# The residual of a state-space block: added by GpSimd in SBUF, or by an identity matmul in the projection's PSUM bank

## The chip, the core and the metric

The kernel runs on one core of a Trainium2 chip. The metric is the device time of one execution in microseconds; of the kernel before it is the median of three runs. A profile is one further execution, recorded by the hardware profiler; its span and its own time are given apart from the median.

## The reference, cut to what matters

Three blocks stand in a row on an input of 4 batches x 1024 positions x 256 channels, all in f32: a gated feed-forward block with three cycles, a state-space (Mamba) block, and the feed-forward block again.

```
x = x + 0.5 * ffn(layernorm(x))
x = x + attn(layernorm(x))
x = x + 0.5 * ffn(layernorm(x))

def attn(resid, ...):                     # resid = layernorm(x)
    xn = resid * rsqrt(mean(resid**2) + eps) * norm_w
    skip, x = xn @ skip_w.T, xn @ in_w.T  # 512 channels each
    x = silu(causal_conv4(x))
    delta = softplus(x @ wd1.T @ wd2.T + wd2_b);  B = x @ wB.T;  C = x @ wC.T
    h[t] = exp(delta[t] * A) * h[t-1] + (delta[t] * x[t]) * B[t]     # 16 states
    y = sum_n h[t, n] * C[t, n] + W_D * x
    y = y * silu(skip)
    return resid + y @ out_w.T
```

So after the state-space block x becomes x + layernorm(x) + y @ out_w.T. The sum of the last two additions is what the change moves.

## The kernel before

The residual stream lies in SBUF all the time as `x_tok`, 32 tiles of 128 positions x 256 channels. The state-space block (function `mamba`) works through 8 segments of 512 positions, numbered i = 0 to 7, two to a batch; the second one of a batch (odd i) starts from the state that the first one left. A segment has 32 units, K = 32 i + k: 16 states n for the first half of the channels and 16 for the second. One unit is, on two channel groups of 128 x 512:

- ScalarE: exp(delta * A) into the PSUM pair `a_bank` (L848, `decay`), and in even segments a copy of the last column (L860)
- GpSimd (POOL): `u` = dx * B (L969, `drive`), up to four units ahead of the scan (a ring of four buffers)
- VectorE (DVE): the scan along the positions (L1065), and in 11 of 16 states the product with C (L1077, result `hc`); in the other five, n = 0, 3, 6, 9, 12, the scan writes `hid` and POOL forms the product (L981, result `hc_pool`)
- TensorE (PE): adds the products over n in the PSUM pair `y_bank` by matmuls with the identity (L1229).

Between the units stand the steps that prepare the next segment and finish the last one. Every engine is programmed by a loop over K, and the tables `AT` and `PLACES` say in which unit k of a segment a step is issued. No scheduler moves anything: an engine does its list in order and waits on semaphores. These steps matter here:

- k = 1, DVE `finish` (L1087) multiplies `y_bank` by the gate for the second channel half of the segment before; with that its `y` is complete.
- k = 2, PE starts the next sum with `feed_through` (L1217), which waits for that `finish`, and then does the output projection of the segment before (kind "out", L1206): for c = 0 (k = 2) and c = 1 (k = 3) two tiles of 128 positions each, 4 matmuls of 256 columns per tile, into one of the two work banks `w_bank`.
- k = 4 and 5, ScalarE `take_out` (L942) copies the bank, 128 x 512, into the scratch `th`.
- k = 7 and 8, POOL `out_add` (L1008) adds `th` to two tiles of `x_tok`.
- k = 5, 6, 8, 9, PE does the input projection of the next segment (kind "in", L1192), k = 7 to 11 ScalarE (L901, L903) takes it out of the bank, and from k = 6 on DVE convolves it (L1100, `convolve`).
- k = 6 and 9, ScalarE `standardise` (L870) replaces x by x + layernorm(x) in `x_tok` for the next segment (semaphore `z`).

The number k tells in which turn of an engine's own loop a step is issued; ScalarE and POOL run ahead of DVE, and PE runs behind it.

An f32 matmul shows as two records in the trace, so the 16 matmul calls of one "out" of a segment are 32 records. After the last segment a drain turn (i = 8) does `finish`, "out", `take_out` and `out_add` for segment 7, with nothing else to do but statistics on DVE; then all engines meet at a barrier, and the second feed-forward block starts.

Of the kernel before, what the change touches and what calls it, by code (L numbers as in the profile page):

```python
# [14 lines left out]
ALU = mybir.AluOpType  # L15
ACT = mybir.ActivationFunctionType
AX = mybir.AxisListType

P = 128
# [606 lines left out]
def mamba(nc, mem, bc_rows):  # L626
# [52 lines left out]
        "dx": (30, 6),  # L679
        "out_add": (7, 8),  # L680
    }

    def due(k, kind):

        return [c for c, t in enumerate(AT[kind]) if t == k]
# [7 lines left out]
    def puts_out(i):  # L693
        return i >= 1
# [41 lines left out]
    with ExitStack() as ctx:  # L736
# [45 lines left out]
            "brow0", "brow1", "brow2", "crow0", "crow1", "crow2",  # L782
            "u", "a", "scan", "carry", "hc", "hc_pool", "y_dve", "y_pool", "y", "out_there", "out_added")}
        block = ctx.enter_context(nc.Block())
# [5 lines left out]
        def col(key, c, n=1):  # L790
            o = W512[key][0]
            return w512[:, c, o:o + n]
# [32 lines left out]
        def _(act):  # L825
# [105 lines left out]
            def gate_half(i, c):  # L931
                b = work_there((i, "skip", c))
                if c == 0:
                    act.wait_ge(S["out_added"], 2 * i)
                if c >= 2:
                    act.wait_ge(S["gated"], i * KE + c - 1)
                nc.scalar.activation(th[:, c % 2, :], b, ACT.Tanh, scale=0.5).then_inc(S["tanh_s"], 1)

            def take_out(i, c):
                b = work_there((i, "out", c))  # L940
                act.wait_ge(S["gated"], i * KE)
                nc.scalar.activation(th[:, c, :], b, ACT.Copy).then_inc(S["out_there"], 1)  # L942

# [15 lines left out]
        def _(pool):  # L959
# [42 lines left out]

            def out_add(i, g):

                pool.wait_ge(S["out_there"], 2 * (i - 1) + g + 1)
                pool.wait_ge(S["z"], 2 * i)
                at = (i - 1) * HT + 2 * g
                nc.gpsimd.tensor_tensor(x_tok[:, at:at + 2, :], x_tok[:, at:at + 2, :],  # L1008
                                        th[:, g, :].rearrange("p (a d) -> p a d", d=DIM),
                                        ALU.add).then_inc(S["out_added"], 1)  # L1010

            for K in range(-UNITS, TOTAL + UNITS):
                i, k = K // UNITS, K % UNITS
                if core(i):
                    drive(K)
                if 0 <= K - WEIGH_LAG < TOTAL and by_pool(K - WEIGH_LAG):
                    weigh(K - WEIGH_LAG)
                for g in due(k, "out_add") if puts_out(i) else ():
                    out_add(i, g)
                if core(i):  # L1020
                    softplus(i, 1, k)
                if prep(i):
                    softplus(i + 1, 0, k)

        @block.vector
        def _(dve):
# [135 lines left out]

            dve.wait_ge(S["out_added"], 2 * 2 * HALVES)
            for t in range(2 * BT):
# [7 lines left out]
        def _(pe):  # L1172
            pe.wait_ge(S["diag_d"], 1)

            def work(i, kind, c, part):
# [23 lines left out]
                elif kind == "dt":  # L1199
                    pe.wait_ge(S["proj"], p + 1)  # L1200
                    op = nc.tensor.matmul(b, w64[:, c * P:(c + 1) * P], proj[0:RANK, :], start=True, stop=True)
                elif kind == "out":
                    pe.wait_ge(S["y"], KE * i)
                    for d in range(KE):
                        at = (2 * c + part) * P
                        op = nc.tensor.matmul(b[:, part * DIM:(part + 1) * DIM], gate[:, d, at:at + P],  # L1206
                                              col("out", d, DIM), start=d == 0, stop=d == KE - 1)
                if part == len(PLACES[kind][c]) - 1:
# [95 lines left out]
```

## Time and profile before

| | |
|---|---|
| median of 3 runs | 1491.64 us (1488.38 to 1492.56) |
| the profiled execution | 1491.21 us, its span 1489.4 us |
| busy share of the span | DVE 88%, PE 77%, POOL 69%, ScalarE 52% |
| the state-space block | about 235 to 1288 us of the span |
| one segment in the middle | about 124.5 us |
| "out" matmuls, copies, POOL additions | 256 records, 16 and 16 |

The span is the time in which the engines work; the 1.8 us between it and the execution's time lie outside. Busy shares are means over stages: the feed-forward blocks at both ends are bound otherwise than the eight segments.

### The profile page before, as it was taken

What the parts mean: (1) busy time and instruction counts of PE and PEld (TensorE: products, weight loads), DVE (VectorE), ACT (ScalarE), POOL (GpSimd) and SP (SyncE); (2) the same over time, 40 slices, a digit from 0 to 9 for tenths busy, and PEclk for the clock granted to TensorE, in tenths of its full rate; (3) what the DMA queues carried; (4) which work ended last, traced back from release to release, by engine and by line L of the source; (5) the groups of instructions that cost most, each with busy time, mean ns of one, the idle gap of its engine ahead of it and who ended that gap; (6) DMA issues with size and microseconds to landing.
All of it is one profiled execution on the core that took longest, in us unless ns stands there. A gap on an engine that the chain in (4) does not pass through costs nothing. (4 is left out here: it accounts for less than half of the span.)

```text
span 1489.4 us, 11591 instructions
## 1 busy us (share of the span) xinstructions
PE 1140.8 (77%) x3072; PEld 537.1 (36%) x3072; DVE 1308.7 (88%) x1793; ACT 776.0 (52%) x1348; POOL 1032.9 (69%) x470
## 2 busy tenths in 40 slices
PE   2979965469687787867868777786887677798996
PEld 2545442123242242333324324232432322454544
DVE  5897894499999989999998999999899899789777
ACT  1544434656754655764565575466557334254443
POOL 1241310698997899899799799879979999224131
PEclk8999986589998998998999899799989989799998
DMA  5000000334434433443343443344344443000001
GB/s 184 0 1 0 0 1 14 115 113 149 161 116 136 148 128 128 142 141 114 128 146 125 141 141 115 139 143 141 114 143 142 141 153 115 1 0 1 29 29 57
DMA packets 46945, 146.53 MB, mean 98 GB/s; under 512 B 4448, under 2 KB 13280, under 8 KB 46880
## 3 DMA queue, kind: packets, MB, share of 16 engines
q1 hardware_dynamic: 46384, 144.96, 29.4%
q10 hardware_dynamic: 496, 0.82, 0.2%
q8 instruction: 25, 0.41, 0.1%
q14 instruction: 40, 0.33, 0.1%
HBM read 141.05 MB, written 4.72 MB: 98 GB/s over the span
## 5 line engine op out<-in xcount | busy, mean ns | idle before, releaser
L969 POOL TENSOR_TENSOR m_u<-m_dx,m_brow 128x1024 f32<-128x1024 f32 x256 | 599.1, 2364 | 36.4 <-DVE m_a_bank L1065 36.3
L1229 PE MATMUL m_y_bank<-m_hc,ident 128*128 128x512 f32 x704 | 382.4, 673 | 188.5 <-DVE m_hc L1077 188.5
L848 ACT ACTIVATE m_a_bank<-m_delta,m_negA 128x512 f32<-128x512 f32 x512 | 335.1, 684 | 174.7 <-DVE m_hc L1077 136.8
L188 POOL TENSOR_TENSOR f_state_lo<-f_state,f_state_hi 128x512 fp32r<-128x512 f32 (+1 forms) x64 | 122.4, 1925 | 251.8 <-DVE f_state_hi L202 251.8
L1229 PEld LDWEIGHTS m_y_bank<-m_hc,ident 128*128 128x128 f32 x704 | 135.3, 207 | 419.1 <-DVE m_hc L1077 293.8
L1065 DVE TENSOR_TENSOR_SCAN m_a_bank<-m_a_bank,m_carry,m_u 128x512 f32<-128x512 f32 x176 | 216.7, 1281 | 12.4 <-POOL m_u L969 12.4
L1077 DVE TENSOR_TENSOR m_hc<-m_a_bank,m_crow 128x512 f32<-128x512 f32 x352 | 224.5, 684 | 0.0
L981 POOL TENSOR_TENSOR m_hc_pool<-m_hid,m_crow 128x1024 f32<-128x1024 f32 x80 | 189.1, 2363 | 49.0 <-DVE m_hid L1065 48.9
L1065 DVE TENSOR_TENSOR_SCAN m_a_bank<-m_a_bank,m_u 128x512 f32<-128x512 f32 x176 | 206.0, 1220 | 10.6 <-POOL m_u L969 9.7
L1229 PE MATMUL m_y_bank<-m_hc_pool,ident 128*128 128x512 f32 x320 | 151.2, 595 | 0.3 <-POOL m_hc_pool L981 0.3
L1192 PE MATMUL m_w_bank<-m_xn,w 128*128 128x512 f32 x240 | 116.9, 610 | 5.5 <-DVE m_x L1124 5.5
L496 ACT ACTIVATE f_h<-f_bank,w 128x512 f32<-128x512 f32 x96 | 66.2, 690 | 88.5 <-PE f_bank L385 88.4
L1065 DVE TENSOR_TENSOR_SCAN m_hid<-m_a_bank,m_u 128x512 f32<-128x512 f32 x80 | 93.6, 1215 | 14.0 <-POOL m_u L969 12.2
L385 PE MATMUL f_bank<-f_state_hi,f_w_lo 128*128 128x512 f32 x192 | 90.3, 470 | 13.0 <-POOL f_state_lo L188 13.0
L1065 DVE TENSOR_TENSOR_SCAN m_hid<-m_a_bank,m_carry,m_u 128x512 f32<-128x512 f32 x80 | 98.3, 1274 | 0.3
L397 PE MATMUL f_bank<-f_h,w 128*128 128x512 f32 x192 | 92.8, 615 | 0.0
L992 POOL TENSOR_TENSOR m_dx<-m_tmp_u,m_dx 128x1024 f32<-128x1024 f32 x16 | 37.8, 2361 | 73.2 <-ACT m_tmp_u L929 73.2
L1229 PEld LDWEIGHTS m_y_bank<-m_hc_pool,ident 128*128 128x128 f32 x320 | 60.3, 190 | 76.8 <-issue 75.0
L385 PE MATMUL f_bank<-f_state_lo,f_w_hi 128*128 128x512 f32 x192 | 78.6, 409 | 0.0
L385 PE MATMUL f_bank<-f_state_hi,f_w_hi 128*128 128x512 f32 x192 | 78.5, 409 | 0.0
L1100 DVE SCALAR_TENSOR_TENSOR m_dx<-m_w_bank,m_conv,m_dx 128x511 f32<-128x511 f32 (+2 forms) x84 | 62.5, 744 | 13.9 <-ACT m_dx L903 12.8
L860 ACT ACTIVATE m_carry<-m_a_bank 128x2 f32<-128x2 f32 x88 | 15.0, 171 | 113.6 <-DVE m_hc L1077 113.6
(132 smaller groups left out, 1606.1 us busy)
## 6 DMA issues: line engine op xcount, KB each, us to landing
m_brow<-bc_rows SPq DMA_DIRECT2D x128, 512.0 KB, 4.8
m_crow<-bc_rows SPq DMA_DIRECT2D x128, 512.0 KB, 4.0
x_tok<-x_in SPq DMA_DIRECT2D x4, 1024.0 KB, 8.7
out<-x_tok SPq DMA_DIRECT2D x3, 1024.0 KB, 4.4
w<-w_in SPq DMA_DIRECT2D x1, 1024.0 KB, 12.3
out<-x_tok SPq DMA_DIRECT2D x2, 512.0 KB, 3.0
w<-w_in SPq DMA_DIRECT2D x1, 750.0 KB, 10.3
w<-w_in ACTq DMA_DIRECT2D x1, 512.0 KB, 6.0
```

The lines of the kernel that those rows point to most:

```text
L188: nc.gpsimd.tensor_tensor(state_lo[:, :, cs], state[:, :, cs], state_hi[:, :, cs].bitcast(F32), ALU.subtract).then_inc(split, 1)
L385: last = nc.tensor.matmul(bank[h * 2 + m][:, :], wt[:, k, m * P:(m + 1) * P], st[:, k, cs], start=n == 0, stop=n == len(passes) - 1)
L397: last = nc.tensor.matmul(bank[4 + h][:, :], w(w256, W256, "w2", k), h1[:, k, h * BANK:(h + 1) * BANK], start=k == 0, stop=k == KD - 1)
L496: nc.scalar.activation(h1[:, m, h * BANK:(h + 1) * BANK], bank[h * 2 + m][:, :], ACT.Gelu, bias=w128[:, o:o + 1]).then_inc(h1_ready, 1)
L848: nc.scalar.activation(a_bank[K % 2][:, j, :], delta[:, i % 2, c, :], ACT.Exp, scale=negA[:, c, n:n + 1]).then_inc(S["a"], 1)
L969: nc.gpsimd.tensor_tensor(u[:, K % U_RING, :, :], dx[:, i % 2, 2 * q:2 * q + 2, :], brow[:, K // 2 % ROW_RING, K % 2, :].unsqueeze(1).to_b ...
L981: nc.gpsimd.tensor_tensor(hc_pool[:, before % POOL_RING, :, :], hid[:, before % POOL_RING, :, :], crow[:, K // 2 % ROW_RING, K % 2, :].uns ...
L1065: nc.vector.tensor_tensor_scan(hid[:, pool_before(K) % POOL_RING, j, :] if by_pool(K) else a, a, u[:, K % U_RING, j, :], 0.0 if i % 2 == 0 ...
L1077: nc.vector.tensor_tensor(hc[:, before % HC_RING, j, :], a_bank[K % 2][:, j, :], crow[:, K // 2 % ROW_RING, K % 2, :], ALU.mult).then_inc( ...
L1100: nc.vector.scalar_tensor_tensor(a[:, s:], b[:, 0:BANK - s], conv[:, c, k:k + 1], a[:, s:], ALU.mult, ALU.add)\
L1192: op = nc.tensor.matmul(b, w256[:, part, o:o + P], xn[:, (p if kind == "in" else i) % 2, part, :], start=part == 0, stop=part == KD - 1)
L1229: op = nc.tensor.matmul(y_bank[:, j, :], ident[:, :], source[:, before % ring, j, :], start=False, stop=K % PASS == POOL_N[-1])
```

## The change

The addition on POOL goes. PE writes the two `x_tok` tiles into the output projection's bank first, by one matmul with the identity for each tile (start=True), and the four matmuls of the projection add to them (start=False). ScalarE's copy then goes from the bank straight into `x_tok`, over the old value. The four identity matmuls of a segment have the shape of the others in this bank: 128 x 128 weights, 256 columns, f32. The semaphore `out_added` goes; what waited for it (the gate's tanh on ScalarE, the final statistics on DVE) waits for `gated` or `out_there`. The wait for `z` moves from POOL's addition to PE's first identity matmul.

```
-        "out_add": (7, 8),
...
             def gate_half(i, c):
                 b = work_there((i, "skip", c))
-                if c == 0:
-                    act.wait_ge(S["out_added"], 2 * i)
-                if c >= 2:
+                if i > 0 or c >= 2:
                     act.wait_ge(S["gated"], i * KE + c - 1)
...
             def take_out(i, c):
                 b = work_there((i, "out", c))
-                act.wait_ge(S["gated"], i * KE)
-                nc.scalar.activation(th[:, c, :], b, ACT.Copy).then_inc(S["out_there"], 1)
+                at = (i - 1) * HT + 2 * c
+                nc.scalar.activation(x_tok[:, at:at + 2, :], b.rearrange("p (a d) -> p a d", d=DIM), ACT.Copy)\
+                    .then_inc(S["out_there"], 1)
...
-            def out_add(i, g):
-
-                pool.wait_ge(S["out_there"], 2 * (i - 1) + g + 1)
-                pool.wait_ge(S["z"], 2 * i)
-                at = (i - 1) * HT + 2 * g
-                nc.gpsimd.tensor_tensor(x_tok[:, at:at + 2, :], x_tok[:, at:at + 2, :],
-                                        th[:, g, :].rearrange("p (a d) -> p a d", d=DIM),
-                                        ALU.add).then_inc(S["out_added"], 1)
...
-            dve.wait_ge(S["out_added"], 2 * 2 * HALVES)
+            dve.wait_ge(S["out_there"], 2 * 2 * HALVES)
...
                 elif kind == "out":
+                    at = (2 * c + part) * P
+                    if part == 0:
+                        pe.wait_ge(S["z"], 2 * i)
+                    nc.tensor.matmul(b[:, part * DIM:(part + 1) * DIM], ident[:, :],
+                                     x_tok[:, (i - 1) * HT + 2 * c + part, :], start=True, stop=False)
                     pe.wait_ge(S["y"], KE * i)
                     for d in range(KE):
-                        at = (2 * c + part) * P
                         op = nc.tensor.matmul(b[:, part * DIM:(part + 1) * DIM], gate[:, d, at:at + P],
-                                              col("out", d, DIM), start=d == 0, stop=d == KE - 1)
+                                              col("out", d, DIM), start=False, stop=d == KE - 1)
```

In the lists below a MATMUL row is one matmul call, and x3 means three alike. On PE, at the units 2 and 3 of a segment, the list before reads:

```order
L1217 MATMUL m_y_bank<-m_x,m_diag_d 128x512 [waits m_y]
L1217 MATMUL m_y_bank<-m_x,m_diag_d 128x512
L1229 MATMUL m_y_bank<-m_hc,ident 128x512 [waits m_hc]
L1229 MATMUL m_y_bank<-m_hc,ident 128x512
L1206 MATMUL m_w_bank<-w,m_gate 128x256 [waits m_y,m_xn]
L1206 MATMUL m_w_bank<-w,m_gate 128x256 x3
L1206 MATMUL m_w_bank<-w,m_gate 128x256 [waits m_y]
L1206 MATMUL m_w_bank<-w,m_gate 128x256 x3
L1229 MATMUL m_y_bank<-m_hc,ident 128x512 [waits m_hc]
```

The same stretch of the changed kernel, whose line numbers are lower by 9 to 13 there (L1193 is the new matmul, L1197 the projection):

```order
L1208 MATMUL m_y_bank<-m_x,m_diag_d 128x512 [waits m_y]
L1208 MATMUL m_y_bank<-m_x,m_diag_d 128x512
L1220 MATMUL m_y_bank<-m_hc,ident 128x512 [waits m_hc]
L1220 MATMUL m_y_bank<-m_hc,ident 128x512
L1193 MATMUL m_w_bank<-x_tok,ident 128x256 [waits m_z,m_xn]
L1197 MATMUL m_w_bank<-w,m_gate 128x256 [waits m_y]
L1197 MATMUL m_w_bank<-w,m_gate 128x256 x3
L1193 MATMUL m_w_bank<-x_tok,ident 128x256
L1197 MATMUL m_w_bank<-w,m_gate 128x256 [waits m_y]
L1197 MATMUL m_w_bank<-w,m_gate 128x256 x3
L1220 MATMUL m_y_bank<-m_hc,ident 128x512 [waits m_hc]
```

Two new matmuls stand at c = 0 and two more at c = 1, all of them ahead of the projection's own and behind the sum of `y_bank`. On POOL, at the units 6 to 9 of a segment, the list before reads:

```order
L1000 TENSOR_TENSOR m_dx<-m_delta,m_x 128x1024 [waits m_delta1]
L969 TENSOR_TENSOR m_u<-m_dx,m_brow 128x1024 [waits m_scan]
L1008 TENSOR_TENSOR x_tok<-x_tok,m_th 128x512 [waits m_z,m_out_there]
L969 TENSOR_TENSOR m_u<-m_dx,m_brow 128x1024 [waits m_scan,m_brow2]
L1008 TENSOR_TENSOR x_tok<-x_tok,m_th 128x512 [waits m_z,m_out_there]
L969 TENSOR_TENSOR m_u<-m_dx,m_brow 128x1024 [waits m_scan]
```

And now:

```order
L998 TENSOR_TENSOR m_dx<-m_delta,m_x 128x1024
L967 TENSOR_TENSOR m_u<-m_dx,m_brow 128x1024 x3
L979 TENSOR_TENSOR m_hc_pool<-m_hid,m_crow 128x1024
```

Both additions are gone, and the three `u` follow each other.

## Rows read from the trace of the kernel before

**Rows 1.** The page: busy us, share of the span, instructions of each engine.
```profile
PE 1140.8 (77%) x3072; PEld 537.1 (36%) x3072; DVE 1308.7 (88%) x1793; ACT 776.0 (52%) x1348; POOL 1032.9 (69%) x470
```
**Rows 2.** Segments 2, 7: length, busy us of PE, PEld, DVE, ACT, POOL, then PEclk, DMA.
```profile
540.00:664.00 124.00, 95.52 (x226) 40.71 (x225) 116.75 (x137) 77.64 (x153) 113.61 (x51) 0.96 0.42 136
1162.00:1288.10 126.10, 94.40 (x218) 42.51 (x216) 111.55 (x149) 42.99 (x68) 103.62 (x47) 0.91 0.33 109
```
**Rows 3.** DVE's waits in segment 2: us in total, times, longest.
```profile
DVE m_gate L1131 <- ACT m_th L937: 2.3, 1, 2.3
DVE m_dx L1100 <- ACT m_dx L903: 2.2, 2, 2.0
DVE m_a_bank L1065 <- POOL m_u L969: 2.1, 2, 1.1
```
**Rows 4.** Timeline of PE, start of segment 2: start, us, what, idle before.
```profile
536.78 1.98 PE L1217 MATMUL m_y_bank<-m_x,m_diag_d 128*128 128x512 f32 x4 [2.28 <-DVE m_gate L1087]
540.32 3.62 PE L1206 MATMUL m_w_bank<-w,m_gate 128*128 128x256 f32 x16
543.78 1.88 PE L1229 MATMUL m_y_bank<-m_hc,ident 128*128 128x512 f32 x4
...
552.38 1.88 PE L1192 MATMUL m_w_bank<-m_xn,w 128*128 128x512 f32 x4
```
**Rows 5.** Timeline of ACT (ScalarE), start of segment 2.
```profile
549.15 0.60 ACT L942 ACTIVATE m_th<-m_w_bank 128x512 f32<-128x512 f32 x1 [3.09 <-PE m_w_bank L1206]
...
554.30 0.84 ACT L901 ACTIVATE m_dx<-m_w_bank,m_spill,m_conv 128x1 f32<-128x1 f32 x3 [0.62 <-PE m_w_bank L1192]
```
**Rows 6.** Timeline of DVE, start of segment 2.
```profile
551.49 2.33 DVE L1065 TENSOR_TENSOR_SCAN m_hid<-m_a_bank,m_u 128x512 f32<-128x512 f32 x2
555.84 2.32 DVE L1100 SCALAR_TENSOR_TENSOR m_dx<-m_w_bank,m_conv,m_dx 128x511 f32<-128x511 f32 x3 [2.02 <-ACT m_dx L903]
```
**Rows 7.** The same place of ACT in segment 1.
```profile
428.91 0.78 ACT L903 ACTIVATE m_dx<-m_w_bank,m_conv 128x512 f32<-128x512 f32 x1 [1.15 <-PE m_w_bank L1192]
```
**Rows 8.** Timeline, start of segment 4: one row of PE, two of DVE.
```profile
790.16 3.05 PE L1229 MATMUL m_y_bank<-m_hc,ident 128*128 128x512 f32 x4
...
803.45 2.34 DVE L1065 TENSOR_TENSOR_SCAN m_hid<-m_a_bank,m_u 128x512 f32<-128x512 f32 x2 [0.88 <-ACT m_a_bank L848]
808.56 1.53 DVE L1100 SCALAR_TENSOR_TENSOR m_dx<-m_w_bank,m_conv,m_dx 128x511 f32<-128x511 f32 x2 [2.77 <-ACT m_dx L903]
```
**Rows 9.** The starts of segments 2 and 4 as stretches, columns as in rows 2.
```profile
536.78:556.50 19.72, 19.72 (x62) 11.86 (x63) 15.57 (x17) 11.05 (x25) 19.72 (x9) 1.00 0.30 97
...
787.80:808.50 20.70, 20.69 (x60) 12.05 (x61) 15.01 (x16) 10.42 (x24) 20.70 (x10) 0.92 0.35 108
```
**Rows 10.** POOL's waits in segment 2.
```profile
POOL m_hc_pool L981 <- DVE m_hid L1065: 6.3, 5, 1.7
POOL m_u L969 <- DVE m_a_bank L1065: 4.1, 2, 2.8
```
**Rows 11.** Timeline, segment 7: two rows of POOL, two of DVE.
```profile
1190.08 1.29 POOL L1008 TENSOR_TENSOR x_tok<-x_tok,m_th 128x512 f32<-128x512 f32 x1
1191.30 2.38 POOL L969 TENSOR_TENSOR m_u<-m_dx,m_brow 128x1024 f32<-128x1024 f32 x1
...
1186.65 2.47 DVE L1065 TENSOR_TENSOR_SCAN m_a_bank<-m_a_bank,m_carry,m_u 128x512 f32<-128x512 f32 x2 [3.23 <-POOL m_u L969]
...
1198.33 2.47 DVE L1065 TENSOR_TENSOR_SCAN m_a_bank<-m_a_bank,m_carry,m_u 128x512 f32<-128x512 f32 x2 [2.12 <-POOL m_u L969]
```
**Rows 12.** The drain turn after segment 7, and the next block's first instruction.
```profile
1278.58 7.15 PE L1206 MATMUL m_w_bank<-w,m_gate 128*128 128x256 f32 x32 [1.53 <-DVE m_gate L1087]
...
1285.77 0.60 ACT L942 ACTIVATE m_th<-m_w_bank 128x512 f32<-128x512 f32 x1 [2.86 <-PE m_w_bank L1206]
1286.44 1.26 POOL L1008 TENSOR_TENSOR x_tok<-x_tok,m_th 128x512 f32<-128x512 f32 x1 [2.19 <-ACT m_th L942]
1288.02 1.28 ACT L490 ACT_TABLE_LOAD   x1 [1.66 <-PEq L736]
```

More of the change, by code:

```diff
@@ L782, in mamba @@
             "brow0", "brow1", "brow2", "crow0", "crow1", "crow2",
-            "u", "a", "scan", "carry", "hc", "hc_pool", "y_dve", "y_pool", "y", "out_there", "out_added")}
+            "u", "a", "scan", "carry", "hc", "hc_pool", "y_dve", "y_pool", "y", "out_there")}
         block = ctx.enter_context(nc.Block())
@@ L1017, in _ @@
                     weigh(K - WEIGH_LAG)
-                for g in due(k, "out_add") if puts_out(i) else ():
-                    out_add(i, g)
                 if core(i):
```

## The prediction, written before the changed kernel was run

> **What bounds the kernel now.** The busy shares of the page come first [rows 1]: DVE 88% of the span, PE 77%, POOL 69%. They are means over three blocks, and the change touches only the middle one, so I split that block into its segments [rows 2]. In segment 2 DVE is busy 116.75 of 124.00 us, POOL 113.61, PE 95.52, ScalarE 77.64. DVE sets the pace, with some 7 us of idle time in a segment, and POOL is close behind. An engine that is not DVE costs time only where DVE waits for it; so the next view is DVE's waits in that segment [rows 3]. There are three kinds: 2.1 us for `u` from POOL, 2.2 us for ScalarE's L903 in front of the convolution, and 2.3 us for the tanh of the gate.
>
> The second of them is where the change lands, and the timelines of the three engines show the chain. PE waits 2.28 us for DVE's `finish`, starts at 536.78 with L1217, and then works without a gap through the 16 records of "out" at c = 0 (540.32), through 4 records of the sum (543.78), through c = 1, and comes to the input projection at 552.38 [rows 4]. ScalarE has waited 3.09 us for the end of "out" c = 1 before its copy, and at 554.30 it has waited again, 0.62 us, for the end of the input projection [rows 5]. DVE starts its convolution only at 555.84, after 2.02 us of idle time that L903 ended [rows 6]. In segment 1 ScalarE's wait for PE in the same place is 1.15 us [rows 7], in segment 4 DVE's wait is 2.77 us [rows 8]. Segments 3, 5 and 6 repeat these patterns. So at the start of each of the segments 1 to 6 the path runs: DVE's finish, PE in one unbroken run, ScalarE, DVE. PE is 23% idle on the whole, but not there.
>
> **What is added on PE.** Four matmul calls with the identity for each "out" of a segment, all within that unbroken run. Their shape is that of the calls beside them, whose 16 records start at 540.32 and are over when the next group starts at 543.78 [rows 4]: 3.46 us, or 0.216 us a record. Four calls are 8 records: 8 x 0.216 = 1.73 us in a segment. The trace has no matmul of `x_tok` with 256 columns, so I bound it. Below: the full-clock price, since an operand of this shape from SBUF is what the neighbours read; I see no reason for less. Above: a stretch at the lower clock, where 4 records of 512 columns take 3.05 us instead of 1.88 [rows 8, 4]; twice the price would be 3.46 us. The run of segment 2 has a granted clock of 1.00, that is 2.4 GHz [rows 9], and each of the twelve groups of 16 "out" records in segments 1 to 6 takes the 3.62 us of rows 4, so I take 1.73.
>
> None of it is hidden in PE's idle time. The first identity matmul stands behind L1217, and that one already waits for `finish`; after it PE is never idle until the input projection is done. So that projection ends 1.73 us later, ScalarE's wait of 0.62 us before L901 stays as it is with everything 1.73 us later, and DVE's idle time before the convolution grows from 2.02 to 3.75 us. There are six segments with both an "out" and a next segment to prepare, i = 1 to 6: **6 x 1.73 = +10.4 us.**
>
> Two things on the way need a look. ScalarE's second copy (549.15) comes 1.73 us later too, and behind it stands the exp for the scan that DVE starts at 551.49 [rows 5, 6]. That scan may then start up to 1 us later, but it has 2.02 us of room before the convolution, which itself moves away by 1.73: nothing more is lost. And nothing behind takes the delay back. The later wait for the tanh [rows 3] hangs on a chain that DVE itself starts with x, through PE and ScalarE, so it shifts with DVE; POOL's `u` runs ahead of DVE by then.
>
> **What is removed on POOL.** Sixteen additions. One takes the engine 1.22 us, from 1190.08 to the start of the next operation at 1191.30 [rows 11], 2.44 us in a segment. In segments 1 to 6 this buys nothing: DVE's waits for `u` lie at units 4 and 5, ahead of the additions at 7 and 8, and from then until the next segment POOL itself idles 6.3 + 4.1 = 10.4 us waiting for scans [rows 10], which swallows anything it is early by. Segment 7 is another matter. It prepares no next segment, so DVE has less to do and overtakes POOL: it waits 3.23 us for `u` at 1186.65 and 2.12 us at 1198.33 [rows 11]. The first wait ends before any addition has run and stays. The second lies behind both; with `u` 2.44 us earlier, the 2.12 us go whole: **-2.1 us.** PE's 1.73 us cost nothing in this segment, since there is no convolution, and the scan that the later exp could hold is followed by the wait of 3.23 us, which takes it in.
>
> **The drain turn.** PE's last 32 records run from 1278.58 to 1285.73, ScalarE copies from 1285.77 for 0.60, POOL adds from 1286.44 for 1.26 until 1287.70, and the next block starts at 1288.02 [rows 12]. Now the first identity matmul runs in the 1.53 us in which PE waits for `finish`; the other three are in the path, 3 x 0.43 = +1.30 us. POOL's addition and the step to it go: from 1286.37 to 1287.70, -1.33 us. Together **0.0 us.**
>
> **Edits at no cost.** ScalarE's copy has the same shape and reads the same bank, with `x_tok` in place of `th`. The wait for `z` that PE takes over was fulfilled a segment before. `gated` in front of the tanh is reached at the end of the segment before, and `out_there` for the final statistics long before the drain.
>
> **The sum.** 10.4 - 2.1 + 0.0 = +8.3 us on the profiled execution's 1491.21 gives 1499.5. The median of the runs shown is 0.4 us higher; on that basis the forecast is 1499.9 us, 0.55% above.
>
> **The rivals.**
>
> *PE's extra work is free, chance 0.11.* For it: PE is 23% idle on the whole, and DVE also has other reasons to stand still near the convolution. The change would then keep only segment 7's gain, -2.1 us: 1489.5. Against it: the 0.62 and 1.15 us for which ScalarE waits for PE right in front of L901 and L903 [rows 5, 7]. If these were put down to the wrong releaser the rival would hold. The Trainium skill ("Perfetto Trace Analysis", Identifying the Most-Contended Engine) says to judge an engine by its occupancy over the trace, and TensorE by the busy share of its weight loads rather than of its matmuls. That share is 36% here, and DVE's is 88%: by that rule one would load PE without a thought and expect this rival's time. The timelines speak against it at this one place, and hence the small chance.
>
> *The clock falls at more starts, 0.14.* In segment 4, after the same 2.28 us of idle time as in segment 2, the clock of the run was 0.92 on average, with the lower level of 1.2 GHz at its beginning [rows 9], and it cost DVE 0.88 + 2.77 - 2.02 = 1.63 us [rows 8, 6]. Segment 6 looks the same, the other four do not. The shift of 1.73 us a segment moves all starts. Dips in all six would add 4 x 1.63 = 6.5 us: 1506.4. Dips in none would take off 3.3 us, 1496.6, and that I count to the forecast. The Trainium skill ("TensorE: Matmul & The Clock Gate", Part 1) has the activity windows free-running, so that the place of a transition in the work changes when the work moves; this fits two starts in six that look alike before the dip, and leaves open which ones are hit next.
>
> *POOL is what bounds, 0.05, and the time falls.* If the 2.44 us that POOL gains in a segment were carried to the next one, and `u` were the last thing that DVE waits for also at the convolution, then 14 additions x 1.22 = 17.1 us would come back: 1474.5. It would need POOL without idle time between the additions and the next segment's units 4 and 5, and rows 10 show 10.4 us of it. The point where it decides is the change of sign: the gain from POOL would have to be more than 1.73 us a segment, of a relief of 2.44.
>
> **How the numbers follow.** Forecast 0.70, clock 0.14, PE free 0.11, POOL 0.05. A measurement of this kernel can tell a difference of about 0.3%, 4.5 us; slower by more starts at 1496.1. The forecast, with its ends at 1496.6 and about 1503, is above that but for 0.02, and the clock rival is wholly: slower 0.82. Within 0.3%: 0.11 + 0.02 = 0.13. Faster 0.05. The range runs from 1493, for a cost on PE that is partly hidden, to 1507, the clock rival's time; what lies outside is PE free and POOL, 0.16. The upper bound of the matmul's price, 3.46 us in a segment, would give 1510.3 and stays outside.
>
> **What would show it.** In the profile after: four more calls in each "out" at 0.216 us a record; DVE's wait for L903 at the convolution near 3.75 us in even segments without a dip, and 1.7 us longer in odd ones; POOL idle about 2.4 us longer in a segment, plus the 1.7 us by which the segment grows; in segment 7 the 3.23 us wait still there and the 2.12 us wait gone; the drain turn as long as before. A segment in the middle takes 126.2 us instead of 124.5. The prediction is wrong if DVE's wait before the convolution does not grow, or if another wait behind it shrinks by as much.

## The result and the profile after

The changed kernel takes 1498.43 us (median of 6 runs, 1495.05 to 1500.5) and the kernel before 1491.69 us (6 runs, 1488.38 to 1493.26): a ratio of 1.0045, 95% interval 1.0030 to 1.0061. That is 6.7 us slower, where +8.3 was forecast. The profiled execution after is 1499.42 us with a span of 1497.6 us, against 1491.21 and 1489.4 before: +8.2 us.

The page's first line, and segment 2 and the unchanged second feed-forward block as stretches (columns as in rows 2):

```profile
PE 1149.5 (77%) x3136; PEld 548.2 (37%) x3136; DVE 1307.6 (87%) x1793; ACT 774.3 (52%) x1348; POOL 1014.0 (68%) x454
```

```profile
540.00:664.00 124.00, 96.62 (x223) 41.94 (x224) 113.08 (x132) 75.13 (x149) 107.49 (x48) 0.96 0.38 130
1299.50:1497.60 198.10, 164.98 (x640) 96.63 (x640) 162.97 (x256) 89.38 (x143) 61.34 (x32) 0.94 0.07 22
```

PE has 64 records more (3072 to 3136), which are 32 calls of two records, and 8.7 us more of busy time. POOL has 16 instructions fewer and 18.9 us less; DVE's work is the same [rows 1]. (Rows 2's stretch is the same piece of time, but the work in it lies later now, by 3.7 us at its start and 7.5 us at its end.) On the page one would say that 19 us of one engine were traded for 9 of another. The time that the calls cost is lost at six places, some 1.7 us at each, and these only the timelines show. PE at the start of segment 2, after:

```profile
540.51 3.39 PE L1208 MATMUL m_y_bank<-m_x,m_diag_d 128*128 128x512 f32 x4 [2.28 <-DVE m_gate L1074]
543.70 2.21 PE L1220 MATMUL m_y_bank<-m_hc,ident 128*128 128x512 f32 x4
545.75 0.59 PE L1193 MATMUL m_w_bank<-x_tok,ident 128*128 128x256 f32 x2
546.18 1.89 PE L1197 MATMUL m_w_bank<-w,m_gate 128*128 128x256 f32 x8
547.91 0.59 PE L1193 MATMUL m_w_bank<-x_tok,ident 128*128 128x256 f32 x2
...
559.53 1.88 PE L1179 MATMUL m_w_bank<-m_xn,w 128*128 128x512 f32 x4
```

The wait of 2.28 us for DVE and the unbroken run behind it are those of rows 4. An identity call holds PE for 0.43 us (545.75 to 546.18, 547.91 to 548.34), two records of 0.216 as forecast. New here is the first row: four records take 3.39 us where they took 1.98 [rows 4]. The granted clock from 540.51 to 543.70 is 0.57 on average, so most of this group ran at the lower level, 1.2 GHz; I call such a place a dip. Of the seven segment starts, two had a dip in the kernel before, those of segments 4 and 6. ScalarE and DVE at the same place:

```profile
550.27 0.60 ACT L939 ACTIVATE x_tok<-m_w_bank 128x512 f32<-128x512 f32 x1 [4.78 <-PE m_w_bank L1197]
...
556.30 0.60 ACT L939 ACTIVATE x_tok<-m_w_bank 128x512 f32<-128x512 f32 x1 [3.95 <-PE m_w_bank L1197]
...
557.05 1.30 ACT L847 ACTIVATE m_a_bank<-m_delta,m_negA 128x512 f32<-128x512 f32 x2
...
561.45 0.83 ACT L900 ACTIVATE m_dx<-m_w_bank,m_spill,m_conv 128x1 f32<-128x1 f32 x3 [0.34 <-PE m_w_bank L1179]
```

```profile
551.84 2.35 DVE L1052 TENSOR_TENSOR_SCAN m_a_bank<-m_a_bank,m_u 128x512 f32<-128x512 f32 x2 [1.22 <-ACT m_a_bank L847]
...
557.88 2.34 DVE L1052 TENSOR_TENSOR_SCAN m_hid<-m_a_bank,m_u 128x512 f32<-128x512 f32 x2 [2.52 <-ACT m_a_bank L847]
...
562.99 2.32 DVE L1087 SCALAR_TENSOR_TENSOR m_dx<-m_w_bank,m_conv,m_dx 128x511 f32<-128x511 f32 x3 [2.77 <-ACT m_dx L902]
```

On ScalarE the operations follow each other in the order of its list. Its second copy waits 3.95 us for PE (3.09 before, [rows 5]), the exp behind it starts only at 557.05, and DVE's scan, which waited for nothing before [rows 6], now waits 2.52 us for that exp. The convolution's wait is 2.77 us. With the waits for `u` (0.97 in this segment, in the place of 2.1 in rows 3) DVE's idle time at this start is 7.48 us and was 4.14: +3.34, of which 1.73 are PE's added work and some 1.6 the new dip of the clock. A start without a dip, segment 1, first DVE's wait at the convolution in the kernel before, then both waits after:

```profile
429.72 0.75 DVE L1100 SCALAR_TENSOR_TENSOR m_dx<-m_w_bank,m_conv,m_dx 128x511 f32<-128x511 f32 x1 [1.07 <-ACT m_dx L903]
```

```profile
428.10 2.46 DVE L1052 TENSOR_TENSOR_SCAN m_hid<-m_a_bank,m_carry,m_u 128x512 f32<-128x512 f32 x2 [0.50 <-ACT m_a_bank L847]
...
432.76 0.75 DVE L1087 SCALAR_TENSOR_TENSOR m_dx<-m_w_bank,m_conv,m_dx 128x511 f32<-128x511 f32 x1 [2.20 <-ACT m_dx L902]
```

```profile
431.94 0.78 ACT L902 ACTIVATE m_dx<-m_w_bank,m_conv 128x512 f32<-128x512 f32 x1 [1.16 <-PE m_w_bank L1179]
```

ScalarE's wait for PE here is what it was, 1.16 us [rows 7], everything 1.7 later; DVE's waits went from 2.82 us to 4.46, of which 1.75 and 1.76 are waits for `u`. The sums at the starts of segments 1 to 6 grow by 1.64, 3.34, 1.63, 1.72, 1.63 and 1.74 us.

Segment 7, DVE:

```profile
1186.90 2.47 DVE L1052 TENSOR_TENSOR_SCAN m_a_bank<-m_a_bank,m_carry,m_u 128x512 f32<-128x512 f32 x2 [0.77 <-POOL m_u L967]
...
1192.50 2.47 DVE L1052 TENSOR_TENSOR_SCAN m_a_bank<-m_a_bank,m_carry,m_u 128x512 f32<-128x512 f32 x2 [1.96 <-ACT m_a_bank L847]
...
1198.53 2.46 DVE L1052 TENSOR_TENSOR_SCAN m_hid<-m_a_bank,m_carry,m_u 128x512 f32<-128x512 f32 x2 [2.39 <-ACT m_a_bank L847]
```

The 2.12 us wait of rows 11 is gone. The 3.23 us wait is gone too, but two waits for ScalarE, 1.96 and 2.39 us, have come: this start has a clock dip as well (PE's first group takes 3.78 us). DVE's waits went from 7.09 to 5.12 us. POOL's waits in segment 2, which answer to rows 10, and the drain turn, which answers to rows 12:

```profile
POOL m_u L967 <- DVE m_a_bank L1052: 8.6, 4, 3.8
POOL m_hc_pool L979 <- DVE m_hid L1052: 7.9, 6, 1.7
```

```profile
1290.11 2.00 PE L1197 MATMUL m_w_bank<-w,m_gate 128*128 128x256 f32 x8 [1.00 <-DVE m_gate L1074]
...
1298.62 0.60 ACT L939 ACTIVATE x_tok<-m_w_bank 128x512 f32<-128x512 f32 x1 [3.72 <-PE m_w_bank L1197]
...
1299.49 1.28 ACT L490 ACT_TABLE_LOAD   x1 [0.27 <-PEq L735]
```

POOL idles 16.5 us in the stretch instead of 10.4: it gave back nothing of what it was relieved of. The drain turn, from DVE's last `finish` to the next block, takes 10.72 us (1288.77 to 1299.49) and took 10.88.

The book over the whole execution: from the `finish` ahead of segment 2 to the one ahead of segment 7 the kernel before needs 629.41 us (535.42 to 1164.83) and the changed one 639.76 (539.18 to 1178.94). Five times 1.73 and one dip more (1.63) make 10.28 of these 10.35. Taken singly the segments agree less well: they grew by 3.74, 1.07, 2.20, 1.14 and 2.20 us, since DVE's wait for the tanh changed too, by 0.4 to 0.5 us up in the even ones and 0.6 to 0.7 us down in the odd ones, which nearly cancels. A segment takes 127.95 us on average and took 125.88 (124.13 to 126.90), not the 124.5 that stands above as its length and from which 126.2 was forecast. The next block starts 11.5 us later than before, and the profile ends only 8.2 later, because the second feed-forward block, with the same code in both, took 198.1 us and not 201.4, at a granted clock of 0.94 and not 0.91.

### The profile page after: what moved, and what is told of

The parts are those of the page before. It is cut to its first block and busy times, and to the rows that moved or that the text cites. A ratio compares the mean times of both kernels' runs of the same rounds, so it can differ in the third digit from the quotient of the medians.

```text
span 1497.6 us, 11677 instructions
## 1 busy us (share of the span) xinstructions
PE 1149.5 (77%) x3136; PEld 548.2 (37%) x3136; DVE 1307.6 (87%) x1793; ACT 774.3 (52%) x1348; POOL 1014.0 (68%) x454
## 5 line engine op out<-in xcount | busy, mean ns | idle before, releaser
L1220 PE MATMUL m_y_bank<-m_hc,ident 128*128 128x512 f32 x704 | 376.0, 663 | 188.1 <-DVE m_hc L1064 188.0
L385 PE MATMUL f_bank<-f_state_hi,f_w_lo 128*128 128x512 f32 x192 | 89.7, 467 | 12.8 <-POOL f_state_lo L188 12.8
## 6 DMA issues: line engine op xcount, KB each, us to landing
w<-w_in SPq DMA_DIRECT2D x1, 750.0 KB, 10.4
```

What stands on the lines that cost most here:

```text
L385: last = nc.tensor.matmul(bank[h * 2 + m][:, :], wt[:, k, m * P:(m + 1) * P], st[:, k, cs], start=n == 0, stop=n == len(passes) - 1)
L1220: op = nc.tensor.matmul(y_bank[:, j, :], ident[:, :], source[:, before % ring, j, :], start=False, stop=K % PASS == POOL_N[-1])
```

## The experiments

The theory, T: the identity matmuls lie in PE's unbroken run at each segment's start and cost their 1.73 us there, six times; what POOL no longer does is worth 2.1 us in segment 7 and nothing elsewhere. Rival R1: PE's work is free and something else made the kernel slower. R2: the path is another one, such as ScalarE's place in the queue. Medians of the kernel before, in the four groups of runs: 1491.38 us for e1, e2, e3 and e5, 1491.74 for e4, e6, e7 and e8, 1489.46 for e9 and e10, 1490.54 for e11 and e12. Each ratio is to the kernel before in its group. The ratios and their intervals are those on record; most are not exactly the quotient of the two medians (e2 1.0080 against 1.0071, e5 1.0125 against 1.0111), so a difference in us that is worked out from a ratio can be a microsecond or two off that of the medians.

**e1: the changed kernel without the residual** (it is left out altogether, the output is another one).

```diff
-                    nc.tensor.matmul(b[:, part * DIM:(part + 1) * DIM], ident[:, :],
-                                     x_tok[:, (i - 1) * HT + 2 * c + part, :], start=True, stop=False)
...
-                                              col("out", d, DIM), start=False, stop=d == KE - 1)
+                                              col("out", d, DIM), start=d == 0, stop=d == KE - 1)
```

> The changed kernel without its identity matmuls: the residual of the state-space block is left out, PE's list is that of the kernel before, POOL has no additions. Path theory (PE's unbroken run at the start of segments 1 to 6 is on the path, POOL's additions are on it in segment 7 alone): DVE's waits in segments 1 to 6 as before, the 2.12 us wait of segment 7 gone, so -2.1 us against before, ratio 0.9985, about 1489.5 us; the drain turn 1.3 us shorter as well, 1488. Rival, POOL bounds: -17 us, ratio 0.989. Rival, the loss of the changed kernel comes from the copy into x_tok or from the moved waits and not from the matmuls: the time stays near the changed kernel's 1498, ratio 1.0045.

Measured: 1489.74 us, ratio 0.9985 (0.9971 to 0.9999), 2.2 us less. With neither POOL's additions nor PE's calls only 0.15% is left. At the starts of segments 1, 4 and 6 DVE's waits are those of the kernel before within 0.01 us. At 2, 3 and 5 they are 1.5 to 1.6 us longer, which was not expected: these starts have a dip in this profile. The drain turn is 1.38 us shorter (9.50), as expected. In segment 7 the wait of 3.24 us stands as in rows 11, and the scans behind it wait for nothing:

```profile
1189.13 2.47 DVE L1052 TENSOR_TENSOR_SCAN m_a_bank<-m_a_bank,m_carry,m_u 128x512 f32<-128x512 f32 x2 [3.24 <-POOL m_u L967]
...
1196.24 2.45 DVE L1052 TENSOR_TENSOR_SCAN m_hid<-m_a_bank,m_carry,m_u 128x512 f32<-128x512 f32 x2
1198.61 2.44 DVE L1052 TENSOR_TENSOR_SCAN m_a_bank<-m_a_bank,m_carry,m_u 128x512 f32<-128x512 f32 x2
```

**e2: the kernel before with the four identity calls added**, each overwritten by the projection that follows.

```diff
+                    nc.tensor.matmul(b[:, part * DIM:(part + 1) * DIM], ident[:, :],
+                                     x_tok[:, (i - 1) * HT + 2 * c + part, :], start=True, stop=True)
                     pe.wait_ge(S["y"], KE * i)
```

> The kernel before, POOL's additions and all, with the four identity matmuls of each out put in front of the projection's; the projection starts the bank anew, so they do nothing to the sum. Path theory: +10.4 us in segments 1 to 6, +1.3 us in the drain turn, nothing in segment 7: +11.7 us, ratio 1.0078, about 1503 us. Rival, PE's extra work is free: ratio 1.000. Rival, only clock dips cost: the middle segments without a dip show DVE's waits as before.

Measured: 1501.97 us, ratio 1.0080 (1.0061 to 1.0099). R1 falls: the calls alone cost more than the whole change. The time holds more than the calls, though: in the profile the state-space block, from the first scan to the start of the next block, is 14.8 us longer than before, with a new dip at the start of segment 2 in it, and what lies ahead of it and behind it, with the same code, is 5.0 us shorter. DVE in segment 2 has the waits of the changed kernel:

```profile
550.01 2.35 DVE L1065 TENSOR_TENSOR_SCAN m_a_bank<-m_a_bank,m_u 128x512 f32<-128x512 f32 x2 [1.21 <-ACT m_a_bank L848]
...
556.04 2.34 DVE L1065 TENSOR_TENSOR_SCAN m_hid<-m_a_bank,m_u 128x512 f32<-128x512 f32 x2 [2.51 <-ACT m_a_bank L848]
...
561.16 1.53 DVE L1100 SCALAR_TENSOR_TENSOR m_dx<-m_w_bank,m_conv,m_dx 128x511 f32<-128x511 f32 x2 [2.78 <-ACT m_dx L903]
```

**e5: the changed kernel with every identity call made twice.**

```diff
                     nc.tensor.matmul(b[:, part * DIM:(part + 1) * DIM], ident[:, :],
+                                     x_tok[:, (i - 1) * HT + 2 * c + part, :], start=True, stop=True)
+                    nc.tensor.matmul(b[:, part * DIM:(part + 1) * DIM], ident[:, :],
                                      x_tok[:, (i - 1) * HT + 2 * c + part, :], start=True, stop=False)
```

> The changed kernel with each identity matmul issued twice, eight calls in an out instead of four. Path theory: another 6 x 1.73 = +10.4 us, drain turn +1.5 us, and segment 7, where the 3.23 us wait for u covered the first four, about +1: +12 to +13 us above the changed kernel, ratio to before near 1.0127, about 1510.5 us. Rival, a fixed cost (a wait, a pipeline break) rather than the matmuls' length: much less than +10. Rival, clock: more PE work keeps the clock up, less than +10.

Measured: 1507.88 us, ratio 1.0125 (1.0102 to 1.0148), 0.0080 or 11.9 us above the changed kernel's (9.5 us between the medians). The start of a segment without a dip shows the price of the calls by itself: in segment 1 DVE's waits are 2.82, 4.46 and 6.17 us with none, four and eight calls, so the cost goes with their number. DVE in segment 5, where the changed kernel has 0.47 us for the exp:

```profile
943.69 2.46 DVE L1052 TENSOR_TENSOR_SCAN m_hid<-m_a_bank,m_carry,m_u 128x512 f32<-128x512 f32 x2 [2.23 <-ACT m_a_bank L847]
...
948.34 0.75 DVE L1087 SCALAR_TENSOR_TENSOR m_dx<-m_w_bank,m_conv,m_dx 128x511 f32<-128x511 f32 x1 [2.19 <-ACT m_dx L902]
```

**e3: the identity only in segment 7 and the drain turn**, POOL's addition in segments 1 to 6. The core of the edit; `th`, `out_add` and `out_added` are as in the kernel before.

```diff
+    def by_pe(i):
+        return i >= 7
...
+                for g in due(k, "out_add") if puts_out(i) and not by_pe(i) else ():
+                    out_add(i, g)
```

> POOL adds for segments 0 to 5 as before; the identity form serves only the out work of segment 7's turn and of the drain turn. Path theory: no cost on PE in segments 1 to 6, the 2.12 us wait of segment 7 gone, the drain turn even: -2.1 us against before, ratio 0.9986, about 1489.6 us. Rival, the POOL relief in segment 7 is taken back by ScalarE waiting for PE's longer run: 0 us.

Measured: 1487.96 us, ratio 0.9976 (0.9963 to 0.9989), 3.6 us less; the 2.1 us lie in the interval. In the profile segment 7 takes 109.82 us and took 112.31, and DVE's waits at its start are 5.11 us, as in the changed kernel. The part of the change that pays is that in segment 7.

**e4: half of the identity work moved to where PE waits.** The residual of c = 0 is one call of 512 columns ahead of the feed-through (L1208), that of c = 1 stays.

```diff
+            def residual(i):
+                use = (i, "out", 0)
...
+                nc.tensor.matmul(bank_of(use).rearrange("p (a d) -> p a d", d=DIM), ident[:, :],
+                                 x_tok[:, (i - 1) * HT:(i - 1) * HT + 2, :], start=True, stop=False)
...
+                if K % UNITS == 2 and puts_out(i):
+                    residual(i)
                 if core(i) and K % PASS == 2:
```

> The changed kernel with the residual of c = 0 (one identity matmul of 512 columns for both tiles, 0.86 us) issued ahead of feed_through, in the 2.3 to 2.7 us in which PE waits for finish; c = 1 as in the changed kernel. Path theory: half of the cost is hidden, -0.86 x 6 = -5.2 us against the changed kernel: about 1493.2 us, ratio to before 1.001. Rival, the cost is a fixed one per out or comes from the clock: as the changed kernel, 1.0045.

Measured: 1491.37 us, ratio 1.0003 (0.9991 to 1.0015). PE and then DVE in segment 2:

```profile
534.12 1.12 PE L1207 MATMUL m_w_bank<-x_tok,ident 128*128 128x512 f32 x2 [0.49 <-ACT m_xn L886]
535.48 1.98 PE L1216 MATMUL m_y_bank<-m_x,m_diag_d 128*128 128x512 f32 x4 [0.23 <-DVE m_gate L1074]
537.30 1.88 PE L1228 MATMUL m_y_bank<-m_hc,ident 128*128 128x512 f32 x4
...
550.29 2.34 DVE L1052 TENSOR_TENSOR_SCAN m_hid<-m_a_bank,m_u 128x512 f32<-128x512 f32 x2
...
555.40 0.75 DVE L1087 SCALAR_TENSOR_TENSOR m_dx<-m_w_bank,m_conv,m_dx 128x511 f32<-128x511 f32 x1 [2.77 <-ACT m_dx L902]
```

Of the 2.28 us in which PE waited for `finish` 0.23 are left, and there is no dip at the start of any segment from 1 to 7. The same number of matmul columns costs 0.0042, 6.3 us, less than in the changed kernel. Both the place and the clock are in this. At the odd starts, which have no dip in either profile, DVE's waits fall from 4.46 to 3.68 us: this is the place, 0.8 us a start, about 5 us for six. At the even starts they fall by 2.6 us, and what this is more, 1.8 us, goes with the dip that is gone. This profile is the fastest of the twelve runs (1487.64 us), so how often the dips are gone in the others isn't known.

**e8: ScalarE's copies one unit later.**

```diff
-        "out_there": (4, 5),
+        "out_there": (5, 6),
```

> The changed kernel with ScalarE's two copies one unit later (5 and 6 instead of 4 and 5), so that an exp stands ahead of each. Path theory with PE as the end of the chain: DVE's waits for exp at the scans of units 5 and 6 (0.5 to 2.5 us) vanish, the wait at the convolution grows by as much, the sum of a segment and the time stay: 1498 us, ratio to before 1.0045. Rival, ScalarE's order is what costs: the time falls by the 0.5 to 3.7 us a segment of these waits, about -12 us, to 1486.

Measured: 1498.15 us, ratio 1.0047 (1.0029 to 1.0065), as the changed kernel. DVE in segment 2:

```profile
550.34 2.33 DVE L1052 TENSOR_TENSOR_SCAN m_hid<-m_a_bank,m_u 128x512 f32<-128x512 f32 x2
...
558.11 1.54 DVE L1087 SCALAR_TENSOR_TENSOR m_dx<-m_w_bank,m_conv,m_dx 128x511 f32<-128x511 f32 x2 [5.44 <-ACT m_dx L902]
```

The waits for the exp, 3.74 us, are gone; the convolution's wait has grown from 2.77 to 5.44, and a wait for `u` of 1.11 us is back, so that the sum at this start is the same within 0.1 us. With this order on PE, the order on ScalarE decides only where DVE's idle time is seen; the end of PE's run decides how much there is. R2 falls for the changed kernel.

**e6 and e7: the input projection of c = 0 between the two halves of "out".** If the projection at the end of PE's run is what DVE's convolution waits for, moving it ahead of "out" c = 1 should take more than the identity costs. e6 has the identity, e7 POOL's addition. The same edit in both (besides, the two banks change places for these uses):

```diff
-        "out": ((2, 2), (3, 3)),
-        "in": ((5, 5), (6, 6), (8, 8), (9, 9)),
+        "out": ((2, 2), (4, 4)),
+        "in": ((3, 3), (6, 6), (8, 8), (9, 9)),
...
-        "out_there": (4, 5),
+        "out_there": (4, 6),
```

> The changed kernel with PE's order at the segment start altered: out c = 0 (unit 2), then the first input projection (unit 3), then out c = 1 (unit 4), with the banks assigned to suit; ScalarE's second copy at unit 6. Path theory: the input projection comes some 5 to 7 us earlier, no longer behind out c = 1; DVE's wait at the convolution falls to what ScalarE's own order leaves (about 1.1 us in even segments as in segment 0, about 0 in odd ones). Against the changed kernel -1.6 to -2.2 us in odd and -4 to -5 in even segments, about -15 us: 1483, ratio to before 0.994. Rival, POOL bounds or DVE waits move elsewhere: less than -5 us.

> The same new order on the kernel before (POOL adds, no identity matmuls). Path theory: DVE's convolution wait falls by 1 to 2.5 us a segment against before, about -8 us: 1484, ratio 0.995; the identity form on top of this order is then 1 to 2 us faster or equal, since its matmuls are covered and segment 7 keeps its gain. Rival: the order gives nothing, ratio 1.000.

Both failed: e6 took 1501.48 us, ratio 1.0076 (1.0058 to 1.0094), and e7 1495.03, ratio 1.0032 (1.0017 to 1.0047). The trace of e7 tells why; PE, ScalarE and DVE in segment 2:

```profile
546.84 1.88 PE L1197 MATMUL m_w_bank<-m_xn,w 128*128 128x512 f32 x4
```

```profile
553.93 0.60 ACT L947 ACTIVATE m_th<-m_w_bank 128x512 f32<-128x512 f32 x1 [4.06 <-PE m_w_bank L1211]
...
556.89 0.82 ACT L906 ACTIVATE m_dx<-m_w_bank,m_spill,m_conv 128x1 f32<-128x1 f32 x3
```

```profile
558.41 0.75 DVE L1105 SCALAR_TENSOR_TENSOR m_dx<-m_w_bank,m_conv,m_dx 128x511 f32<-128x511 f32 x1 [3.27 <-ACT m_dx L908]
```

PE did start the projection early, at 546.84. But ScalarE's second copy waits 4.06 us for "out" c = 1, and L906, whose projection PE had done by about 548.6 (1.7 us after its start), stands behind it and runs at 556.89. I had moved the copy's unit along with the matmuls and not looked at what is queued behind it.

**e9 and e10: the same, with the copy issued behind that work.** e9 is made from e6, e10 from e7 (there `out_add` is at (7, 9) too).

```diff
-        "out_there": (4, 6),
+        "out_there": (4, 7),
...
+                if prep(i):
+                    prepare(i, k)
                 for c in due(k, "out_there") if puts_out(i) else ():
                     take_out(i, c)
-                if prep(i):
-                    prepare(i, k)
```

> The order of e6 (out c = 0, first input projection, out c = 1; identity form), with ScalarE's second copy issued behind its take-out of the first input projection (unit 7) instead of ahead of it (unit 6). Theory from e6 and e7: their loss is ScalarE's queue, in which the copy waited 4 to 6 us for PE with 4.5 us of work and the convolution's input behind it. Then DVE's wait at the convolution falls to under 1.5 us in even and to about 0 in odd segments, against 3.3 to 6.9 and 2.0 to 3.8; the identity matmuls are covered there, and segment 7 keeps its 2.1 us: 7 to 10 us below before, ratio 0.994, about 1483 us. Rival, PE itself is too full for the new order (the second input projection comes late): no gain, ratio 1.00 or above.

> The same order without identity matmuls, POOL adding at units 7 and 9. Theory from e6 and e7: the convolution's wait as in e9 or a little less, segment 7 keeps its 2.1 us wait for u: 5 to 8 us below before, ratio 0.9955, about 1485 us, and not faster than e9. Rival, the identity matmuls still cost on the path in this order: e10 is faster than e9 by more than 3 us.

Measured: e9 1481.92 us, ratio 0.9951 (0.9937 to 0.9964); e10 1481.41, ratio 0.9946 (0.9934 to 0.9959). Both lie where they were expected. In segment 2 of e9 the convolution waits 0.81 us, and its second part, which had not been expected to wait, 1.85:

```profile
555.35 2.32 DVE L1092 SCALAR_TENSOR_TENSOR m_dx<-m_w_bank,m_conv,m_dx 128x511 f32<-128x511 f32 x3 [0.81 <-ACT m_dx L907]
...
563.35 0.75 DVE L1092 SCALAR_TENSOR_TENSOR m_dx<-m_w_bank,m_conv,m_dx 128x511 f32<-128x511 f32 x1 [1.85 <-ACT m_dx L907]
```

The one edit of the queue's order took 0.0125 off the ratio of e6 and 0.0086 off that of e7, 18.6 and 12.8 us. And it turns the question of this change round: in the old order the identity form is 6.7 us slower than POOL's, in this one the two can't be told apart.

**e11 and e12: what both findings give together.** e11 is e10 with `by_pe(i)`, as in e3, so that segment 7 and the drain turn use the identity. e12 is e9 with `residual(i)`, as in e4.

> The kernel of e10 (new order, POOL adds) with the identity form of e3 in the turn of segment 7 and in the drain turn alone. Path theory: e10 with the 2.12 us wait of segment 7 gone, 2.1 us below e10, about 8 us below e9 - 0.4 and 10 us below before: ratio 0.993, about 1480 us against 1490 of before. Rival: the relief is taken back in segment 7 by ScalarE's wait for PE: as e10, 0.9946.

> The kernel of e9 (new order, identity form everywhere) with the residual of c = 0 ahead of feed_through as in e4. Path theory: what is left of the identity matmuls in e9 is DVE's 1.8 us wait at the second convolution of the three even segments; with PE's run 0.86 us shorter it falls by that much: 2.6 us below e9, ratio 0.9935. Rival: the second convolution's wait comes from the clock and stays: as e9, 0.9951.

(e11's difference to e9 is misstated there; meant was 2.1 us below e10.) Measured: e11 1478.12 us, ratio 0.9917 (0.9899 to 0.9935); e12 1478.85, ratio 0.9918 (0.9902 to 0.9934). Both beat the kernel before by some 12 us and the changed one by 0.0128, 19 us; they can't be told apart. e12 is a little faster than its 0.9935. In it the second convolution wait is gone, the whole 1.8 us and not 0.86 of it, and so are the dips that e9 has at all three even starts. So the calls' place and the clock both have a part in this gain, and e12 doesn't separate them. PE's wait for `finish` is down to 0.66 us:

```profile
1036.49 1.98 PE L1221 MATMUL m_y_bank<-m_x,m_diag_d 128*128 128x512 f32 x4 [0.66 <-DVE m_gate L1079]
...
1054.29 2.31 DVE L1092 SCALAR_TENSOR_TENSOR m_dx<-m_w_bank,m_conv,m_dx 128x511 f32<-128x511 f32 x3 [0.81 <-ACT m_dx L907]
1060.42 2.31 DVE L1092 SCALAR_TENSOR_TENSOR m_dx<-m_w_bank,m_conv,m_dx 128x511 f32<-128x511 f32 x3
```

## Why the prediction was right, and where it was off

**The identity calls on the path, +10.4 us: right.** The price of a call is 0.43 us as taken from the records beside it, DVE's waits grow by 1.63 to 1.74 us at five of the six starts, and the five segments between two `finish` come out within 0.1 us of five times 1.73 and one dip. The clean measurement is the start of segment 1, with no dip in any of the three profiles: 2.82, 4.46 and 6.17 us of waits with none, four and eight calls. As totals, 11.7 us were expected of e2 and 12 to 13 of e5, with the drain turn in them; by the ratios both measured 0.0080, 11.9 us (e2's interval is 9.1 to 14.8), by the medians 10.6 and 9.5. They agree, but dips and the clock outside the block are in them as well. The odd starts of e4 show that it is a price of the place.

**Where DVE would wait: the step that was wrong.** I wrote that the convolution's wait in even segments grows to 3.75 us and that the scan behind the exp "may then start up to 1 us later". In fact it is 2.77 us at all three (before, 2.02 in segment 2 and 2.77 in 4 and 6), in the odd ones it grew by 1.1 and not by 1.7, and the scan waits 0.5 us in the odd and up to 2.52 in the even ones: I had moved ScalarE's copy by 1.73 us but gave the exp behind it 1 us only. e8 shows the cost of this mistake to be nothing in time, since the idle time merely moves from one row to another. In e6 the same oversight, work queued behind a copy that waits, cost the whole expected gain. It also spoils the sign that was named: "wrong if DVE's wait before the convolution does not grow". In segments 4 and 6 that wait did not grow, 2.77 to 2.78, and yet the cost is there, at the scans ahead of it. The sign had to be the sum of DVE's waits from `finish` to the convolution.

**POOL's relief, 0 in segments 1 to 6: right.** POOL waits 6.1 us longer for scans in segment 2 than before; 4.1 were named, and the dip adds its 1.6. e1, with neither PE's calls nor POOL's additions, is 2.2 us below the kernel before and not 17, and at its starts without a new dip DVE's waits are unchanged.

**Segment 7, -2.1 us: the sum right, its parts not.** In e1 it is as written: 3.23 stays, 2.12 goes. In the changed kernel's profile a clock dip put two waits for ScalarE in the place of the 3.23; the sum of DVE's waits still fell by 1.97.

**The drain turn, 0.0: right**, 10.88 to 10.72 us.

**The tanh, no change: off by a little, and by the clock.** Over the seven gates (segments 0 to 6) DVE's waits for it add up to 1.4 us more, single ones 0.7 us up or down. The traces take this apart. Ahead of it PE adds one unit to `y_bank` and does eight records of the projection of x (128 x 96 weights), here in segments 1 and 3 of the kernel before, with DVE's wait below each:

```profile
458.37 3.48 PE L1229 MATMUL m_y_bank<-m_hc,ident 128*128 128x512 f32 x4 [3.28 <-DVE m_hc L1077]
461.68 3.60 PE L1197 MATMUL m_w_bank<-m_x,w 128*96 128x512 f32 x8
469.44 0.69 DVE L1131 SCALAR_TENSOR_TENSOR m_gate<-m_th,m_w_bank 128x512 f32<-128x512 f32 x1 [1.08 <-ACT m_th L937]
...
707.85 3.78 PE L1229 MATMUL m_y_bank<-m_hc,ident 128*128 128x512 f32 x4 [2.90 <-DVE m_hc L1077]
711.43 4.88 PE L1197 MATMUL m_w_bank<-m_x,w 128*96 128x512 f32 x8
720.47 0.69 DVE L1131 SCALAR_TENSOR_TENSOR m_gate<-m_th,m_w_bank 128x512 f32<-128x512 f32 x1 [2.63 <-ACT m_th L937]
```

The run takes 6.74 us (458.37 to 465.11) at a granted clock of 0.78 and 8.29 us (707.85 to 716.14) at 0.63, 1.55 us more, and the wait is 1.55 us longer. In the changed kernel the two runs take 7.46 and 7.60 us and the waits are 1.79 and 1.95. In segments 1 to 6 of all 14 profiles the wait is the length of this run less 5.66 us in odd and less 5.30 us in even segments, to within 0.01 us, whatever was edited. So this wait is a second place in each segment where a dip costs DVE time, one for one, and the forecast counted dips at the starts only.

**The clock: the likeliest case and its rival both came in part.** Dips stood at the starts of 4 and 6, and now at 2, 4, 6 and 7, so at three of the six starts that count and not at two or all six. A new one costs what rows 6 and 8 said, about 1.6 us (segment 2: 3.34 less 1.73). Which starts are hit isn't explained by anything measured here.

**The total.** The profile shows +11.5 us up to the start of the last block, 3.2 us over my sum: 1.6 for the dip, 0.6 ahead of the state-space block, 1.4 in segments 0 and 1, whose tanh waits are 0.60 and 0.71 us longer, less 0.5 in segment 7 and the drain. The last block, whose code is the same, gave 3.3 back by the clock it was granted. The difference of the medians, 6.7 us (interval 4.5 to 9.1), holds the 8.3. That the profiled execution came out 8.2 us longer, as if the sum of 8.3 had been met to 0.1, is luck: the state-space block itself grew by 10.9 us, and the last block's clock took the surplus back.

## What to carry to other kernels

An engine that is 23% idle has no free time at a place where it runs without a gap between one wait and the next: price added work by that run, and look for the wait ahead of it as the place to put it (e4, at its starts without a dip). Before moving a matmul, follow the copy that takes its result through the in-order queue of its engine and ask what is ready behind it (from e7 to e10, 12.8 us). Relief for an engine that itself waits for the bottleneck is worth nothing (e1), except in the stage where it is the one waited for (e3).

## What the runs showed of the hardware

**Unchanged code varies from execution to execution.** Over all 14 profiles, the second feed-forward block, with the same instructions in each, lasts 197.9 to 201.5 us. Its granted clock goes with this, but not strictly: the six at 0.94 take 197.9 to 198.1 us, the five at 0.91 take 201.3 to 201.5, but for one (e10) at 198.8. The first scan of the state-space block lies 277.1 to 282.4 us from the start, though nothing ahead of it was changed; there the granted clock, 0.85 to 0.89, does not order the times. A difference of 3 us between two profiles is thus not a finding before it is placed in a block, and two traces are best compared from a common mark.

**Filling PE's idle time at a segment's start took dips away.** In e4 and e12 none of the starts of segments 1 to 7 has one (the first group takes 1.98 us at each), where the kernel before has two and the changed one four. In both, a call of 512 columns fills part of the 2.28 us ahead of the run. That this is the cause, and not the other shifts that the edit brings, wasn't tested by itself.
